# Moving two copies of ScalarE in the second step of a middle layer's round

## The reference

```python
sa = _mha(x, x, x, tgt_mask, ...)                    # 16 heads of 16
x = _ln(x + sa, ln1_g, ln1_b)
ca = _mha(x, enc_output, enc_output, memory_mask, ...)
x = _ln(x + ca, ln2_g, ln2_b)
ff = relu(x @ ff_w1 + ff_b1) @ ff_w2 + ff_b2         # 256 -> 1024 -> 256
x = _ln(x + ff, ln3_g, ln3_b)
```

## Time and profile before

| | |
|---|---|
| median of 3 runs | 3384.29 us (3381.09 to 3385.19) |
| profiled execution | 3386.52 us, its span 3384.8 us |
| PE busy | 3052.0 us, 90% of the span |
| DVE busy | 2036.9 us, 60% |
| ACT busy | 1909.7 us, 56% |
| POOL busy | 1491.7 us, 44% |

### The profile page before, as it was taken

One profiled execution on the slowest core, in us unless ns is written; L12 is line 12 of the kernel. 1 busy time (PEld: TensorE's weight loads), 2 busy tenths in 40 slices (PEclk: granted clock), 3 DMA queues, 4 the chain that ended last, 5 costly groups with the idle time before them and its releaser, 6 DMA issues. The chain is left out here.

```text
span 3384.8 us, 82099 instructions
## 1 busy us (share of the span) xinstructions
PE 3052.0 (90%) x28400; PEld 2668.3 (79%) x28400; DVE 2036.9 (60%) x4306; ACT 1909.7 (56%) x7826; POOL 1491.7 (44%) x1874
## 2 busy tenths in 40 slices
PE   7999999599999999727999999999999999848886
PEld 5999998379999999625888888888888888745664
DVE  2545554244444444325777777888878778726665
ACT  2444444234444444325777777777777777617775
POOL 1223423103445444611555555555555555543444
PEclk8999999799999999858999999999999999979998
DMA  3222121410111110032222222333211121122321
GB/s 104 63 75 68 62 93 38 143 35 29 54 53 53 53 35 28 35 117 82 77 74 71 73 73 70 91 95 111 64 61 61 61 62 56 33 81 83 88 88 57
DMA packets 218094, 232.77 MB, mean 69 GB/s; under 512 B 41920, under 2 KB 183232, under 8 KB 215360
## 3 DMA queue, kind: packets, MB, share of 16 engines
q1 hardware_dynamic: 217920, 230.49, 21.6%
HBM read 148.57 MB, written 65.01 MB: 63 GB/s over the span
## 5 line engine op out<-in xcount | busy, mean ns | idle before, releaser
L1736 ACT ACTIVATE middle_stage<-middle_psum,middle_neg_max 128x128 f32<-128x128 f32 x2048 | 728.0, 392 | 344.6 <-DVE middle_neg_max L1716 344.4
L1736 ACT ACTIVATION_READ_ACCUMULATOR middle_stage<-middle_psum,middle_neg_max 128x1 f32 x2048 | 473.4, 231 | 0.0
L1716 DVE TENSOR_REDUCE middle_neg_max<-middle_psum 128x4 f32<-128x512 f32 x512 | 338.1, 682 | 64.9 <-PE middle_psum L1679 63.2
L1690 PE MATMUL middle_psum<-middle_eye,middle_stage 128*128 128x128 f32 x2048 | 320.5, 279 | 18.6 <-DVE middle_stage L1722 8.6
L1690 PEld LDWEIGHTS middle_psum<-middle_eye,middle_stage 128*128 128x128 f32 x2048 | 231.2, 142 | 72.0 <-issue 46.4
L1645 POOL TENSOR_TENSOR middle_attended_lo<-middle_mix,middle_attended_hi 128x256 fp32r<-128x256 f32 x128 | 95.0, 742 | 433.9 <-DVE middle_attended_hi L1728 433.9
L536 POOL TENSOR_TENSOR cross_ff_hidden_lo<-cross_ff_relu,cross_ff_hidden_hi 128x256 fp32r<-128x256 f32 x128 | 100.9, 789 | 279.9 <-DVE cross_ff_hidden_hi L531 279.9
L97 PE MATMUL middle_psum<-middle_n_yt_hi,middle_w_lo 128*128 128x256 f32 x640 | 193.7, 303 | 14.1 <-ACT middle_n_y L1853 12.5
L1946 POOL TENSOR_TENSOR middle_ff_hidden_lo<-middle_ff_relu,middle_ff_hidden_hi 128x256 fp32r<-128x256 f32 x256 | 183.4, 737 | 49.0 <-DVE middle_ff_hidden_hi L1940 49.0
L1722 DVE COPY middle_stage<-middle_psum 128x512 f32<-128x512 f32 x256 | 175.6, 686 | 15.6 <-PE middle_psum L1690 15.3
L1617 ACT ACTIVATE fourth_stage<-fourth_psum,fourth_neg_max 128x128 f32<-128x128 f32 x512 | 182.1, 387 | 3.4 <-DVE fourth_neg_max L1593 3.4
(11 more groups left out here) (346 smaller groups left out, 10915.8 us busy)
## 6 DMA issues: line engine op xcount, KB each, us to landing
middle_stage<-middle_a_k SPq DMA_DIRECT2D x1024, 16.0 KB, 1.8
middle_xt_hi<-x_hi SPq DMA_DIRECT2D x32, 256.0 KB, 2.7
middle_xt_lo<-x_lo SPq DMA_DIRECT2D x32, 256.0 KB, 3.0
middle_ct_hi<-context_hi SPq DMA_DIRECT2D x32, 256.0 KB, 2.9
middle_ct_lo<-context_lo SPq DMA_DIRECT2D x32, 256.0 KB, 3.2
middle_x_rows<-x_rows SPq DMA_DIRECT2D x32, 256.0 KB, 2.8
middle_mask_flags<-flags SPq DMA_DIRECT2D x128, 64.0 KB, 1.9
x_rows<-middle_n_z SPq DMA_DIRECT2D x32, 256.0 KB, 2.2
```

Source lines behind the costliest of these rows:

```text
L1690: ins = pe.transpose(banks.psum[:, TURN_BANK, x * SEQ:(x + 1) * SEQ], self.sh.p_wide[:, 4 * b + t, x, :], self.sh.eye[:])
L1716: dve.tensor_reduce(self.sh.neg_max[:, 4 * b + t, :], psum[:, SCORE_BANKS[t], :].rearrange("p (x k) -> p x k", x=4), AX_X, ALU.max, negate ...
L1736: ins = act.activation(self.sh.p_wide[:, 4 * b + t, x, :], psum[:, SCORE_BANKS[t], x * SEQ:(x + 1) * SEQ], ACT.Exp, bias=self.sh.neg_max[: ...
```

## The change

All of it is in step x1. On ACT the cast of the second norm's high part goes away, and the spread copy moves from behind the second group of exponentials to behind the fourth. On DVE that cast is added ahead of the low part, and the weighing moves behind the step's last copy of a turn.

```diff
@@ ACT, step x1
                 exp(x1_next, 1)
                 if ok(-2):
                     norm2.act(act, Back(r, 2), psum)
-                    norm2.act_hi(act, Back(r, 2))
-                spread(x1)
                 exp(x1_next, 2)
...
                 exp(x1_next, 3)
+                spread(x1)
                 if stream.is_last(r):
                     layer.act_swap(act, "v1")
@@ DVE, step x1
                 turned(x1[1], 2)
                 if ok(-2):
+                    norm2.dve_hi(dve, Back(r, 2))
                     norm2.dve_lo(dve, Back(r, 2))
+                turned(x1[1], 3)
                 norm(x1[0])
-                turned(x1[1], 3)
```

## The result

The changed kernel took 3408.47 us (median of 4 runs, 3403.46 to 3410.82) against 3384.11 us for the kernel before (4 runs, 3381.09 to 3385.19): a ratio of 1.0068, with an interval of 1.0056 to 1.008. It is slower, by 24 us in the medians where 14.3 were forecast; 3398.6 was the forecast, and 3408.5 stands at the very edge of the range, half a microsecond above the 3408 that was written. The profiled execution took 3403.46 us, its span 3401.7, which is 16.9 above that of the kernel before.

What follows compares the result with a forecast made beforehand. PE was taken as the bound, with little time to spare over DVE at turn 1. Losses of 15 × 0.72 and 14 × 0.25 us made 14.3, giving 3398.6 us against the median; range 3386 to 3408 us.

Steps and rivals of the forecast that it cites:

- The score waits close, the exponentials move up by 0.96: ACT x1: exponentials start 0.96 us earlier, so PE's waits for them at y0's scores (11.8 + 10.8 us) close.
- DVE idles for the spread copy: DVE x1: the weighing waits 1.36 us for ACT's later spread copy, delaying first maximum and copy of turn 0.
- PE's first hidden product ... is not delayed: DVE x1: despite the added cast the low part starts 0.19 us earlier, so PE's product needing it is not late.
- The collision with the residual: y0: DVE's hidden casts wait 0.27 us for POOL's residual; the second cast may be held up to 0.52 more.
- The loss a round: PE's turn 1 in y0 comes late: 0.72 us a round without the mask, 0.25 in the masked layer.
- Fill, swaps and the end: Fill, drain and weight-swap rounds are priced like neighbouring rounds, with an error of 1 or 2 us.
- The sum: Whole kernel: 15 × 0.72 + 14 × 0.25 = 14.3 us slower, 3398.6 us against the median; chance 0.40.
- both casts held: Rival, y0: POOL holds both hidden casts, 0.52 us more in some rounds; 3406 us; chance 0.13.
- the gap closes and nothing takes its place: Rival: both score waits of PE vanish, 22.6 us won, with no new wait; 3361.7 us; chance 0.10.
- No collision: Rival, y0: DVE is late but its casts miss the residual's hold; 6.5 us lost, 3390.8 us; chance 0.25.
- Absorbed delay: Rival: turn 1's lateness eats PE's 8.9 us wait for the norm's columns; 5.4 us lost, 3389.7 us; chance 0.12.
- POOL's work 1.8 us later, at nothing, since POOL idles long stretches: POOL's low part, residual and inverse rows come 1.8 us later, costed at nothing; PE needs inverse rows only behind turn 1.

Runs made afterwards that it cites:

- the cast alone: Kernel before with only the second norm's high-part cast moved from ACT to DVE: 3369.0 us, ratio 0.9939; repeated 3366.17 us, 0.9934.
- the second set of medians: The changed kernel run again unaltered, beside other runs on the same chip: 3410.38 us (4 runs), ratio 1.0062 to the kernel before.
- the run with the late residual: Changed kernel with POOL's residual moved behind the low parts of the first hidden blocks of y0: 3398.59 us, ratio 1.0033.
- The last two runs: Changed kernel with x1's weighing behind y0's hidden casts, 3403.63 us (1.0047); or behind y0's first maximum and copy of turn 0, 3442.58 us (1.0145).
- the weighing behind the statistics: Changed kernel with DVE's weighing of x1 set behind the third norm's statistics, ahead of the hidden casts: 3393.59 us, ratio 1.0017.

## Why the prediction was right, and where it was short

- **The score waits close, the exponentials move up by 0.96.** Right: 1.86 to 0.90 us from the columns, 22.6 us of waits to 1.2.
- **DVE idles for the spread copy.** 1.36 predicted, 1.30 measured.
- **"PE's first hidden product ... is not delayed".** True, and PE even did these products 0.14 us faster, as under the cast alone; in the changed kernel this wins nothing, since turn 1 waits for DVE all the same.
- **The collision with the residual.** Its place was right, its size too small. 0.27 was taken, the bound was 0.79, and 0.38 came (0.87 − 0.49). The residual's hold was counted, the meeting of the second cast with the rows of the inverse sums was only put in the bound; the rows fit that meeting, but no run took it away alone. In the earlier trace rows as here, the price was read best from the pair of instructions together.
- **The loss a round.** In the second middle layer turn 1 came 0.87 us later after the columns, 0.72 predicted; the waits lasted 1.61 where the prediction said about 1 us, although its own loss of 0.72 and the 0.67 closed ahead make 1.4. In the masked layer two turns 1 are 45.03 apart (2018.54 to 2063.57) where the kernel before had 44.67: 0.36, 0.25 predicted. Of the surplus of 0.11 to 0.15 a round, 0.11 is the collision's again (0.38 − 0.27). So 14 × 0.36 + 15 × 0.87 = 18.1 us.
- **Fill, swaps and the end, "priced like their neighbours, an error of 1 or 2 us".** The remainder to 20.3 us is theirs, 2.2: at the swap in the middle turn 1 waits 2.45 us, in the last round 2.99.
- **The sum.** 14.3 predicted, 20.3 in the stretch, 24 in the medians of four runs. The direction and the path were right, the size was too small. The 4 us between the last two lie outside the stretch and differ between executions (3403 to 3411 for one kernel); the second set of medians gives a ratio of 1.0062. What makes an execution reach the middle layers some us sooner or later was not tried and stays open. That the time still touches the range owes something to luck: its upper end came from the rival with both casts held, which holds only in part.
- **The rivals.** That the gap closes and nothing takes its place: the cast alone comes near it, with 6.3 of 22.6 us of waits left and a stretch 21.1 shorter. No collision: the run with the late residual shows what that would have been, +12.2 us in the stretch where the rival counted 6.5. Absorbed delay: the wait for the columns kept its 8.5 us. Both casts held: partly true, and its time, 3406, is the nearest to what came.
- **"POOL's work 1.8 us later, at nothing, since POOL idles long stretches".** True for this change (DVE waits once for POOL's rows, 1.3 us), but the reason given was wrong. The last two runs show that the idle stretch lies ahead of that work: a further 0.85 us of lateness against the scores (the low part starts 1.02 after them here, 1.87 with the weighing behind the statistics) makes DVE wait for POOL in 28 rounds.

The Trainium skill, "SBUF — State Buffer", Who interferes with whom, names casts among the instructions of VectorE that contend with GpSimd. The runs agree, at two places (0.49 to 0.87 beside the residual, 0.49 to 1.05 beside the low part), and show that each goes when POOL's instruction is elsewhere, here to 0.49 and 0.50.

## What to carry to other kernels

A cast that waits only for its own data may be moved to an engine that idles there; but a copy on which another engine's queue depends must not be put behind work that this queue doesn't need, for everything behind the waiting instruction is late with it. When a step is moved, follow the queues of all the engines that it feeds to their next idle stretch, and price whatever comes to lie beside it: here POOL's share of 44% hid a chain with less than 0.85 us of slack. How far a listed wait falls is not what a move wins, since work ahead of it can become quicker too: compare starts, counted from the same instruction. Where two executions of one kernel differ by more than the term in question, measure between the same two instructions in both traces.

## What was not expected of the hardware

- Two casts of 128x256 on DVE (0.49 us) took 0.87 beside an addition of 128x512 on POOL and 1.05 beside a subtraction of 128x256 that itself took 0.74. The shorter instruction of POOL cost more (0.56 against 0.38). It began at 2467.36, 0.16 us after the first of the two casts; the second began 0.04 after it and took 0.85 us, where one such cast takes 0.28 to 0.29 in rows that show it singly:

```profile
2467.40 0.85 DVE L1940 CAST middle_ff_hidden_hi<-middle_ff_relu 128x256 fp32r<-128x256 f32 x1
```

- That second cast thus met nearly the whole of POOL's 0.74 us, while the residual of 1.29 us was two thirds over when the casts of the changed kernel came.
- The maximum of 128x512 out of PSUM on DVE took its 0.68 us also where it ran beside POOL's work, as at 2478.86 above, beside the rows of the inverse sums.
- Between the same two instructions, 1334 us apart, two executions of one kernel on two occasions agreed to 0.1 us, while their whole spans differed by 4.6.
